# Sorting edges into bins: a sum of four tiles in place of the scan, and half of the slot one-hots on ScalarE

## What is computed

```
h = max(layernorm(x), 0);  x = x + L0(h, edge_index, ...)      # messages with attention, 2 steps
h = max(layernorm(x), 0);  x = x + L1(h, edge_weight, ...)     # weighted means in both directions, a GRU
h = max(layernorm(x), 0);  x = x + L2(h, edge_index, edge_attr_4, ...)  # 4 edge kinds, 4 GRU steps
h = max(layernorm(x), 0);  x = x + L3(h, edge_index, edge_type_16, ...) # 16 relations
```

## Time and profile before

| | |
|---|---|
| median of three runs | 8124.99 us (8105.39 to 8125.53) |
| the profiled execution's own time | 8105.65 us |
| its span in the trace | 8103.9 us |
| TensorE busy | 5879.0 us (73%) |
| VectorE busy | 3552.1 us (44%) |
| ScalarE busy | 1759.6 us (22%) |

### The profile page before, as it was taken

The page is one execution under the profiler, slowest core; times in us unless marked ns, Lnnn a source line. Parts: engine busy times, 40 slices in busy tenths (PEclk is TensorE's granted clock), DMA queues, the critical chain, the costliest instruction groups (busy, mean ns, idle before and its releaser), DMA issues. The chain is left out here.

```text
span 8103.9 us, 101737 instructions
## 1 busy us (share of the span) xinstructions
PE 5879.0 (73%) x31333; PEld 4125.2 (51%) x31441; DVE 3552.1 (44%) x7349; ACT 1759.6 (22%) x4298; POOL 2379.4 (29%) x2471
## 2 busy tenths in 40 slices
PE   1437777666666777666678979899998995666665
PEld 1334444466666656666664434444444442656555
DVE  6889999455555445555546521211212115111111
ACT  0006665233333333333330110100101012000000
POOL 0000000456666445556640000000000000666665
PEclk8669999888888888888888989999999997555555
DMA  1005555333333333333336445354453533111111
GB/s 49 1 11 209 205 206 199 102 100 100 100 101 101 82 93 100 101 100 102 101 83 229 180 162 192 129 192 150 170 191 130 191 129 136 45 44 45 44 45 43
DMA packets 418896, 951.03 MB, mean 117 GB/s; under 512 B 61905, under 2 KB 274310, under 8 KB 408582
## 3 DMA queue, kind: packets, MB, share of 16 engines
q1 hardware_dynamic: 314502, 681.10, 24.5%
q0 software_dynamic: 104192, 267.02, 12.1%
HBM read 741.69 MB, written 206.20 MB: 117 GB/s over the span
## 5 line engine op out<-in xcount | busy, mean ns | idle before, releaser
L1484 POOL DMA_INDIRECT ring<-rows,stage x1632 | 1596.8, 978 | 2017.0 <-issue 1060.0
L1555 PE MATMUL ps<-here,spread 128*128 x3264 | 1104.6, 469 | 836.8 <-DVE ring L1514 574.2
L1374 POOL DMA_INDIRECT ring<-rows,stage x808 | 771.1, 954 | 3073.1 <-ACT stage L1358 2660.2
L1151 PE MATMUL ps<-strip,trans_part 128*128 128x512 f16 (+1 forms) x8400 | 1643.1, 357 | 14.2 <-DVE trans_part L1114 14.2
L1151 PEld LDWEIGHTS ps<-strip,trans_part 128*128 128x128 bf16 x8400 | 780.6, 98 | 928.2 <-issue 62.4
L1555 PEld LDWEIGHTS ps<-here,spread 128*128 128x128 f32 x3264 | 659.9, 224 | 960.3 <-issue 891.1
L1514 DVE TENSOR_TENSOR ring<-ring,ps 128x512 f32<-128x512 f32 x816 | 560.6, 687 | 1255.5 <-remote 626.7
L1412 PE MATMUL ps<-ring,mark 128*128 128x128 f32 x1616 | 628.3, 488 | 380.2 <-DMA ring<-rows,stage 249.2
L1573 PE MATMUL ps<-ring,mark 128*128 128x128 f32 x3264 | 777.8, 329 | 0.0
L1573 PEld LDWEIGHTS ps<-ring,mark 128*128 128x128 f32 x3264 | 653.6, 223 | 66.4
L1110 DVE TENSOR_TENSOR trans<-ps,be 128x512 f32<-128x512 f32 x100 | 69.2, 692 | 1302.8 <-PE ps L1137 1302.8
(11 more groups left out here) (289 smaller groups left out, 6183.6 us busy)
## 6 DMA issues: line engine op xcount, KB each, us to landing
strip<-adj SPq DMA_DIRECT2D x400, 800.0 KB, 4.4
adj<-piece SPq DMA_DIRECT2D x125, 640.0 KB, 3.1
locs<-loc_rows SPq DMA_DIRECT2D x420, 128.0 KB
ahead<-ahead_piece SPq DMA_DIRECT2D x125, 320.0 KB, 2.1
back<-back_piece SPq DMA_DIRECT2D x125, 320.0 KB, 2.4
sheet<-ahead SPq DMA_DIRECT2D x25, 1600.0 KB, 8.6
sheet<-back SPq DMA_DIRECT2D x25, 1600.0 KB, 7.3
ring<-rows,stage POOLq DMA_INDIRECT x2440
```

Source lines behind the costliest of these rows:

```text
L1151: last = eng.matmul(k.ps[:, b, 0:cols], part[:, s % TABLES, m, t * D:(t + 1) * D], strip[:, n % RING, c0:c0 + cols], start=n == 0 and m == ...
L1374: eng.indirect_dma_start(ring[:, t, :], None, rows, bass.IndirectOffsetOnAxis(stage[:, t:t + 1], 0)).then_inc(s_full[q], 16)
L1484: eng.indirect_dma_start(ring[:, t, :], None, rows, bass.IndirectOffsetOnAxis(stage[:, t:t + 1], 0)).then_inc(s_full[q], 16)
L1555: last = eng.matmul(hid[:, j, :], spread[:, q, t * P:(t + 1) * P], here[:, bass.ds(cols[t] * 2, W2)], start=True, stop=True)
```

## The change

The order of the rank's sum changes, and half of the one-hots are made on another engine.

- The one-hot of the bin is made once, column by column (36 x 26, three buffers with a column of zeros ahead); `hot`'s bin-by-bin layout and the scan are gone. `twos` adds each column of it to the one ahead, `fours` adds `twos` two columns apart, so a column of `fours` is the sum of four columns.
- TensorE's count is one matmul by `lower` and then, per bank, matmuls by `all_one` on `fours` shifted by 1, 5, 9, ... columns, which add up all earlier columns: 16 matmuls with 5,382 columns in all, where four with 1,800 stood.
- `rank` is reduced over the innermost dimension, not over a strided one.
- VectorE makes the one-hots of the first 18 columns in one instruction. Those of the last 18 are made by ScalarE, `ones_of(w)`: per column |slot - rank| (`apart`, 128 x 256), and per six columns relu(1 - that) (`other`, 128 x 1536). The permutation takes 36 matmuls from the one and 36 from the other.
- `binned` is bf16, not fp32.

```diff
-            binned = k.sb("binned", [P, WORDS, NW, NW, 2], F32, inner)
+            binned = k.sb("binned", [P, WORDS, NW, NW, 2], BF16, inner)
...
-                eng.tensor_tensor(hot[:, w % 3, :, :], own_bin[:, :, 0].unsqueeze(1).to_broadcast([P, NW, J]), window[:, :, :],
-                                  ALU.is_equal).then_inc(s_hot, 1)
+                eng.tensor_tensor(in_pairs(hot[:, w % 3, :, :]), every(window_j, J),
+                                  own_bin[:, :, :].unsqueeze(2).to_broadcast([P, J, NS // 2, 2]), ALU.is_equal).then_inc(s_hot, 1)
                 eng.wait_ge(s_hot, w + 1)
+                c.step(eng.tensor_tensor(twos[:, 2:2 + J, :], hot[:, w % 3, :, :], hot_all[:, w % 3, 0:J, :], ALU.add))
                 if w >= 2:
                     eng.wait_ge(s_cnt, w - 1)
-                    eng.wait_ge(s_perm, CHUNKS * (w - 1))
-                eng.tensor_tensor_scan(flat(run, w % 2), keep[:, :, :].rearrange("p s j -> p (s j)"),
-                                       flat(hot, w % 3), 0.0, ALU.mult, ALU.add).then_inc(s_run, 1)
-                c.step(eng.tensor_tensor(in_pairs(hot_j[:, w % 2, :, :]), every(window_j, J),
-                                         own_bin[:, :, :].unsqueeze(2).to_broadcast([P, J, (NW + 1) // 2, 2]), ALU.is_equal))
+                    eng.wait_ge(s_perm, 2 * (w - 1))
+                eng.tensor_tensor(fours[:, w % 2, :, :], twos[:, 2:2 + J, :], twos[:, 0:J, :], ALU.add).then_inc(s_run, 1)
...
-                d.step(eng.tensor_reduce(rank[:, :], picked[:, :, :].rearrange("p s j -> p j s"), AX.X, ALU.add))
-                d.step(eng.tensor_copy(rank16[:, :, :], rank[:, :].unsqueeze(2).to_broadcast([P, J, 2])))
-                for ch in range(CHUNKS):
-                    n = w * CHUNKS + ch
-                    if n >= 3:
-
-                        eng.wait_ge(s_perm, n - 2)
-                    eng.tensor_tensor(in_pairs(place[:, n % 3, :, :]), every(slot_no, CH),
-                                      rank16[:, ch * CH:(ch + 1) * CH, :].unsqueeze(2).to_broadcast([P, CH, SLOT // 2, 2]),
-                                      ALU.is_equal).then_inc(s_place, 1)
+                if w >= 2:
+
+                    eng.wait_ge(s_apart, CH * (w - 1))
+                d.step(eng.tensor_reduce(rank[:, w % 2, :], picked[:, :, :], AX.X, ALU.add))
+                d.step(eng.tensor_copy(rank16[:, :, :], rank[:, w % 2, 0:CH].unsqueeze(2).to_broadcast([P, CH, 2])))
+                if w >= 2:
+
+                    eng.wait_ge(s_perm, 2 * (w - 2) + 1)
+                eng.tensor_tensor(in_pairs(place[:, w % 2, :, :]), every(slot_no, CH),
+                                  rank16[:, :, :].unsqueeze(2).to_broadcast([P, CH, SLOT // 2, 2]), ALU.is_equal).then_inc(s_place, 1)
...
+                    last = eng.matmul(k.psf[:, at + a:at + b], lower[:, :], flat(hot, w % 3)[:, a:b], start=True, stop=False,
+                                      skip_group_check=True)
+                    for gap in range(NS, b, 4 * NS):
+                        lo = max(a, gap)
+                        last = eng.matmul(k.psf[:, at + lo:at + b], all_one[:, :], flat(fours, w % 2)[:, lo - gap:b - gap],
+                                          start=False, stop=gap + 4 * NS >= b, skip_group_check=True)
...
-                for ch in range(CHUNKS):
-                    n = w * CHUNKS + ch
-                    eng.wait_ge(s_place, n + 1)
+                for ones, s_ones, per in ((place, s_place, 1), (other, s_other, CH // CUT)):
+                    eng.wait_ge(s_ones, per * (w + 1))
...
+            def ones_of(w):
+
+                eng.wait_ge(s_dve, 4 * w + 2)
+                for c in range(CH // CUT):
+                    n = w * (CH // CUT) + c
+                    if n >= 2:
+                        eng.wait_ge(s_other, n - 1)
+                    for i in range(CUT):
+                        j = CH + c * CUT + i
+                        eng.activation(apart[:, n % 2, i, :], slot_no[:, :], ACT.Abs, bias=rank[:, w % 2, j:j + 1],
+                                       scale=-1.0).then_inc(s_apart, 1)
+                    if w >= 2 and c == 0:
+
+                        eng.wait_ge(s_perm, 2 * (w - 1))
+                    eng.wait_ge(s_apart, (n + 1) * CUT)
+                    eng.activation(other[:, w % 2, c * CUT:(c + 1) * CUT, :], apart[:, n % 2, :, :], ACT.Relu,
+                                   bias=k.ones[:, 0:1], scale=-1.0).then_inc(s_other, 1)
+
+            eng.wait_ge(s_set, 4)
+            ones_of(0)
             for w in range(NW):
-                eng.wait_ge(s_perm, CHUNKS * (w + 1))
+                if w + 1 < NW:
+                    ones_of(w + 1)
+                eng.wait_ge(s_perm, 2 * (w + 1))
```

More of the change, by code:

```diff
@@ L540, in sort_bins @@
     nc = k.nc
-    F = NW * J
-    M = WORDS * (NW + 1)
-    CH = 12
+    NS = NW + 1
+    F = NS * J
+    M = WORDS * NS
+    CH = J // 2
     words, bins = k.words, k.bins
     own_bin = k.sb("own_bin", [P, J, 2], F16, own)
-    window = k.sb("window_no", [P, NW, J], F16, own)
-    window_j = k.sb("window_row", [P, NW + 1], F16, own)
-    hot_j = k.sb("hot_row", [P, 2, J, NW + 1], BF16, own)
+    window_j = k.sb("window_row", [P, NS], F16, own)
+    hot_all = k.sb("hot_row", [P, 3, 1 + J, NS], BF16, own)
+    hot = hot_all[:, :, 1:1 + J, :]
+    twos = k.sb("hot_twos", [P, 2 + J, NS], BF16, own)
+    fours = k.sb("hot_fours", [P, 2, J, NS], BF16, own)
     slot_no = k.sb("slot_no", [P, SLOT], BF16, own)
@@ L552, in sort_bins @@
     all_one = k.sb("all_one", [P, P], BF16, own)
[L553 to L558, removed]
+    picked = k.sb("picked", [P, J, NS], F32, own)
+    rank = k.sb("rank", [P, 2, J], F32, own)
+    rank16 = k.sb("rank16", [P, CH, 2], BF16, own)
     over = k.sb("over", [P, J], F32, own)
     past = k.sb("past_all", [P, NW], F32, own)
-    word = k.sb("word", [P, 2, J, WORDS, NW + 1], BF16, own)
-    place = k.sb("place_hot", [P, 3, CH, SLOT], BF16, own)
+    word = k.sb("word", [P, 2, J, WORDS, NS], BF16, own)
+    place = k.sb("place_hot", [P, 2, CH, SLOT], BF16, own)
+    other = k.sb("place_other", [P, 2, CH, SLOT], BF16, own)
+    CUT = 6
+    apart = k.sb("slots_apart", [P, 2, CUT, SLOT], BF16, own)
     names = ("s_set", "s_hot", "s_run", "s_cnt", "s_word", "s_place", "s_perm", "s_bin",
-             "s_dve", "s_over", "s_ovs", "s_first")
+             "s_dve", "s_over", "s_ovs", "s_first", "s_apart", "s_other")
     (s_set, s_hot, s_run, s_cnt, s_word, s_place, s_perm, s_bin, s_dve, s_over,
-     s_ovs, s_first) = (k.sem(x) for x in names)
-    flat = lambda t, i: t[:, i, :, :].rearrange("p s j -> p (s j)")
-    CHUNKS = J // CH
+     s_ovs, s_first, s_apart, s_other) = (k.sem(x) for x in names)
+    flat = lambda t, i: t[:, i, :, :].rearrange("p j s -> p (j s)")
     PERM = 4
@@ L573, in _ @@
         def _(eng):
-            eng.iota(window[:, :, :], [[1, NW], [0, J]], 0, 0, allow_small_or_imprecise_dtypes=True).then_inc(s_set, 1)
-            eng.iota(window_j[:, :], [[1, NW + 1]], 0, 0, allow_small_or_imprecise_dtypes=True).then_inc(s_set, 1)
+            eng.iota(window_j[:, :], [[1, NS]], 0, 0, allow_small_or_imprecise_dtypes=True).then_inc(s_set, 1)
             eng.iota(slot_no[:, :], [[1, SLOT]], 0, 0, allow_small_or_imprecise_dtypes=True).then_inc(s_set, 1)
-            eng.memset(keep[:, :, :], 1.0).then_inc(s_set, 1)
-            eng.wait_ge(s_set, 4)
-            eng.memset(keep[:, :, 0:1], 0.0).then_inc(s_set, 1)
+            eng.memset(hot_all[:, :, 0, :], 0.0).then_inc(s_set, 1)
+            eng.memset(twos[:, 0:2, :], 0.0).then_inc(s_set, 1)
         @block.vector
@@ L583, in _ @@
             c = Count(eng, s_first)
-            c.step(eng.tensor_scalar(lower[:, :], k.before[:, :], -1.0, None, ALU.add))
+            c.step(eng.tensor_copy(lower[:, :], k.before[:, :]))
             c.step(eng.memset(all_one[:, :], 1.0))
@@ L619, in _ @@
                 q = k.psf[:, (w % 2) * 2 * BANK:(w % 2) * 2 * BANK + F]
[L620 to L631 removed]
+                d.step(eng.tensor_tensor(picked[:, :, :].rearrange("p j s -> p (j s)"), q, flat(hot, w % 3), ALU.mult))
+                if w >= 2:
[6 more added lines that the diff above has]
+                                  rank16[:, :, :].unsqueeze(2).to_broadcast([P, CH, SLOT // 2, 2]), ALU.is_equal).then_inc(s_place, 1)
+                d.step(eng.tensor_scalar(over[:, :], rank[:, w % 2, :], float(SLOT), 0.0, ALU.is_ge, ALU.add,
                                          accum_out=past[:, w:w + 1]))
@@ L659, in _ @@
                     eng.wait_ge(s_bin, w - 1)
-                for ch in range(CHUNKS):
-                    n = w * CHUNKS + ch
-                    eng.wait_ge(s_place, n + 1)
+                for ones, s_ones, per in ((place, s_place, 1), (other, s_other, CH // CUT)):
+                    eng.wait_ge(s_ones, per * (w + 1))
                     for i in range(CH):
-                        j = ch * CH + i
+                        j = i if ones is place else CH + i
```

(2 more changed lines are left out.)

8 lines of the change are left out of this document (3 added, 5 removed).

## The result

The changed kernel took 8231.92 us (median of four runs, 8216.05 to 8247.98) against 8122.34 before (four runs, 8105.39 to 8125.53): slower by 110 us, ratio 1.0141 with a 95% interval of 1.0124 to 1.0159. 8245 was forecast, with a range from 8190 to 8280. Its profiled execution took 8221.38 us, with a span of 8219.3 in the trace.

The account below looks back on a forecast made before the run. VectorE, with a small wait behind TensorE, was taken to bound the sort; a serial chain would add 124 us, start -5.6, end +13.9: +132 on 8105.65, 8238, with half the 19 us median difference 8245; range 8190 to 8280.

Parts of the forecast that it names:

- The chain: Sort window, rank to rank: ScalarE, TensorE's second half and VectorE run in series, 22.4 us instead of 17.0.
- The prices: Sort instructions: 256-element activation 0.49 us alone, six 2.54, Relu of 1536 1.57, dense reduction 1.13.
- the rival with the dearer ScalarE: Sort: activations don't overlap or the reduction stays at 1.73; window 23.0 to 24.2 us, total 8260 to 8290; chance 0.15.
- The clock: Permutation's second half on TensorE: clock falls in an idle of over 5 us, so 36 matmuls take 4.1 us.
- clock up: Permutation's second half runs at 2.4 GHz: 2.25 us instead of 4.1, window 20.5, total 8195 to 8205; chance 0.2.
- The ends: Sort's start up to rank(0) gains 5.6 us; its end from rank(23) to the last copies loses 13.9.
- the prediction's own list of signs against it: Whole kernel: wrong if `fours` starts without a wait, a ScalarE piece takes under 3 us, or another stage moved.
- Faster: Sort: ScalarE's part lies beside VectorE's, window 12.8 us, gain 101 less the end, total 8015 to 8030; chance 0.05.

Follow-up runs that it names:

- the one that put it into the old kernel: Kernel before, with its scan and four count matmuls, plus ScalarE making the last 18 columns' one-hots and bf16 `binned`: 8252.26 us, ratio 1.0230.
- the filler: Changed kernel plus 76 unused matmuls of 88 columns on TensorE between the permutation's halves, numbers come out wrong: 8162.68 us, ratio 1.0114.
- the last chip: Chip where the changed kernel was rerun unchanged beside the kernel before and the fastest one: changed 7509.88 us, ratio 1.0107.
- the sums alone: Changed kernel with all one-hots back on VectorE in three chunks with three buffers, new count, dense reduction and bf16 `binned` kept: 7984.90 us, ratio 0.9892.

## Why the prediction was right

**The chain.** The sum of one window was 12.2 (ScalarE) + 4.1 (36 matmuls) + 5.83 (VectorE) + 0.3 = 22.4. Measured: 12.16, 4.08, 5.63 (292.95 to 298.58) and 0.2: 22.1. The largest miss is VectorE's 0.2, from `fours` to the first product. The two runs that cut the chain in different places, a third buffer (22.1 to 13.11) and fewer columns on ScalarE (22.1 to 15.83), and the one that put it into the old kernel (17.02 to 24.85), each came within 0.6 us of the sum made for it.

**The prices.** An activation of 256 took 494 ns (0.49), six of them 2.50 (2.54), the Relu of 1536 1575 ns (1.57), the dense reduction 1128 ns (1.13). The activations do overlap, so the rival with the dearer ScalarE falls, and the reduction did leave its strided price. The prediction also weighed a price without that gain, which it drew from the Trainium skill's one mode for all reductions (VectorE: DVE Perf Modes, "The perf-mode tier table"). The two rows, 1735 ns for 900 strided and 1128 for 936 dense, show a gain; one mode does not make one price.

**The clock.** The low level in the second half was right in 21 of 25 windows, and for the reason given: the idle between the halves. With the filler in it the clock was up for the second half in all but four windows. The case of the rival *clock up* is what the filler's run built, and it gave 20.3 where 20.5 stood.

**The ends and the total.** Start -6.9 for -5.6, end +14.7 for +13.9. Of the end's 0.8, 0.65 is the doubled copy to `binned`, which the prediction took at its old price. The windows gave +115 for +124. The sum of the terms was +132, the sort measured +122, the medians differ by 110. The profiles show 12 us less in layer 0, which I had held fixed; another stage that moves was on the prediction's own list of signs against it, and this one did, by 12 us here and by 83 on the last chip. So the mechanism in the sort was right, and the total holds two misses in the same direction, 10 us in the sort and 12 in layer 0. That 8245 lies only 13 over the median is in part luck: it takes half of the 19 us between the median of before and its profiled run, for no reason that a run shows (and the half on 8238 makes about 8248), where the whole would have made 8257.

**The rivals on the other side.** *Faster* needed ScalarE's part beside VectorE's and not in the chain. That is what the third buffer does, and the price given for that case, 12.8 a window, was 13.11 when it was built. The mechanism was real; the changed kernel did not have the buffer that it takes.

## What to carry to other kernels

Handing half of a step to an idle engine helps only if its part is not in the loop that returns to the first engine. Before counting busy time, follow the wait that reuses a buffer: which iteration must be finished, which engine finished it last, and what is queued behind the waiting instruction. If that closes a circle within one iteration, the engines' times add up; one more buffer, so that the circle spans two iterations, turned a loss of 1.4% into a gain of 1%. That gain, though, is no more than the sums alone gave with everything left on VectorE (ratio 0.9899 and 0.9892 on one chip). Only fitting the handed-over part to the free time (12 columns instead of 18) made the idle engine pay: 11.43 us a window where all on VectorE takes 13.18.

## What the runs showed of the hardware that I had not expected

- A ScalarE copy of 128 x 125 from PSUM took 428 ns with an fp32 destination whose elements lie 200 bytes apart, and about 910 ns with a bf16 one 100 bytes apart (medians of 908 to 919 in eleven profiles).
- A VectorE reduction that reads fp32 at steps of 144 bytes took 1735 ns for 900 elements, a dense one 1128 ns for 936.
- The same gathers of layer 0 took 976 to 1037 ns on the mean in different kernels, and the kernel before took 8122, 8068, 7454 and 7441 us on four chips. Between the first and the last, in their profiles, 491 us of the spread lie in layer 0 (2757 and 2266 from its first to its last attention) and some 170 in layer 3, the other one that gathers.
